# Moving four products with 1/l, a copy and a normalisation within the issue order of VectorE and ScalarE, in a fused attention and recurrent layer

## The chip, the cores and the metric

The kernel runs on one core of a Trainium2 chip. The metric is the device time of one execution in microseconds (us), lower is better. A profile is one execution recorded by the hardware profiler.

## What is computed

The input x has 32 batch elements of 256 tokens with 128 features. First comes an attention layer with 16 heads of 64, causal, with four learned key and value rows ahead of the tokens, then a gated recurrence over the 32 batch elements. Both have a layer norm before them and a residual sum behind them.

```python
# attention, on h = rms_norm(layernorm(x)) * norm_weight
q, k, v = split(h @ w_qkv.T)              # q and k are rotated (rope)
k, v = concat([persist_mem, k]), concat([persist_mem, v])
attn = softmax(where(causal, q @ k.T * 64 ** -0.5, min))
x = x + (attn @ v) @ w_out.T
# recurrence over t = 0..31, on z = layernorm(x)
f, i = sigmoid(z[t] @ wf.T + c @ uf.T + bf), sigmoid(z[t] @ wi.T + c @ ui.T + bi)
c = f * c + i * tanh(z[t] @ wc.T + c @ uc.T + bc)
x = x + tanh(z @ wo.T + c_final @ uo.T + bo)
```

## The kernel before, in words

**Iterations and steps.** Each engine runs its own list of instructions; semaphores tie the lists together. Every list is `body(j, p)` for j = 0 to 34, and each body has eight steps s = 0 to 7, one for each pair of heads. Four batch elements are in work at once. In iteration j the element j is projected and rotated, and its scores for the row maxima are made. Element j - 1 has its transposed scores, exponentials and products with V. Element j - 2 is divided by the softmax sums l, projected by w_out, added to x and normalised for the second layer. Element j - 3 goes through the recurrence's gates. The order of the calls in a step is written out by hand and is the order in which the engine takes them; an engine whose next instruction waits does nothing else.

**TensorE's list** (`body`, L1211), by step: `project(j, s)` (six matmuls, L971, the first instructions of each step with the exception of a transpose in steps 3 and 7); at step 0 `transpose_xn` (L1130), which waits for the second norm; at step 5 `transpose_x` (L938); at step 6 `values(j, 0)` (L990), which waits for `h_lo_done` and fills `ps_work`; at steps 5 and 6 `project_out` for two quarters each (L1115). Quarter n waits for product n + 1 of the element with 1/l (`norm_done`): `project_out(j-2, 0)` and `(1)` in step 5, `(2)` and `(3)` in step 6. Then in each step the scores for the maxima (L1010), the transposed scores (L1034 to L1061), and `attend(j-1, s-1)` (L1078), the product with V. `attend` writes the one bank `ps_pv`, so it waits for `raw_done`, the copy of the pair before it.

**ScalarE's list** (L626): in step s, behind the copies that open some steps, `exp(j-1, s)` (L535), then `hi(j, s-1)`, the fp16 copy of the rotated pair (L520), which waits for GpSimd's `rope_add(j, s-1)`; then `raw_copy(j-1, s-1)` (L560), the copy of `ps_pv`, which waits for `attend(j-1, s-1)`; in step 7 `second_norm(j-2)` (L616) comes last. It waits for the factors that GpSimd's `rstd` makes (L404 to L410). `h_high(j+1)` (L471) stands at the head of step 5.

**VectorE's list** (L864): in step s `rotate(j, s)` (L770 and L771, products with cos and sin out of PSUM), then at step 5 `h_low(j+1)` (L714), which waits for `h_high`, then `maxima` (L781). `divide(j-2, n)` (L817) multiplies two pairs of `raw` by `rinv`, both in SBUF. Products 0 and 1 stand at the end of step 4, behind `state(j-3, 1)` (L858); products 2 and 3 at the end of step 5. The factors 1/l are spread by DMAs (`spread_linv`, L298) into `rinv`.

**GpSimd's list** (L412): in step s `rope_add(j, s-1)` (L396), which adds the two rotated parts when a DMA on the sync engine's queue (`swap`, L280) has swapped the rows of one; in step 7 `rstd(j-2)`; then `prob_add(j-1, s)` (L389), behind the exponential of the step. All of these read SBUF.

Of the kernel before, what the change touches and what calls it, by code (L numbers as in the profile page):

```python
# [5 lines left out]
NB, NT, D = 32, 256, 128  # L6
# [3 lines left out]
NPAIR = NH // 2  # L10
# [41 lines left out]
def build(nc, x, x_last, w_qkv_t, w_out_t, norm_w, pm_k, pm_v, ffn_w, ffn_b, bo_row, consts_f32, consts_cast,  # L52
# [9 lines left out]
    with ctx:  # L62
# [135 lines left out]
        def real(b):  # L198

            return not isinstance(b, int) or 0 <= b < NB  # L200
# [245 lines left out]
        def _(act):  # L446
# [179 lines left out]
            def body(j, p):  # L626
                a, b, c, d = real(j), real(j - 1), real(j - 2), real(j - 3)
                for s in range(NPAIR):
                    if s == 3 and b:
                        copy_top(j - 1, 1)  # L630
                    if s == 7 and a:
                        copy_top(j, 0)
                    if s == 4 and real(j + 4):
                        load_batch(j + 4)
                    if s == 0 and d:
                        xt_high(j - 3)
                    if s == 1 and d and j - 3 == NB - 1:
                        gate_tanh_last(j - 3)
                    elif s in (1, 2) and d and j - 3 < NB - 1:
                        gate_tanh(j - 3, s - 1)  # L640
                    if s < 2 and j == 1:
                        end_values(s)
                    if s in (3, 4) and b:
                        value_copy(j - 1, s - 1)
                    if s == 5 and real(j + 1):
                        h_high(j + 1, 1 - p)
                    if s == 6 and a:
                        value_copy(j, 0)
                    if s == 7 and a:
                        value_copy(j, 1)  # L650
                    if b:
                        exp(j - 1, s)
                    if s == 0 and b:
                        hi(j - 1, NPAIR - 1)
                    if s >= 1 and a:
                        hi(j, s - 1)
                    if s == 1 and b:
                        end_keys(j - 1, 1)
                    if s == 6 and a:
                        end_keys(j, 0)  # L660
                    if s == 0 and c:
                        raw_copy(j - 2, p, NPAIR - 1)
                    if s >= 1 and b:
                        raw_copy(j - 1, 1 - p, s - 1)
                    if s == 2 and real(j + 1):
                        first_norm(j + 1)
                    if s == 5 and d:
                        state_high(j - 3)
                    if s == 7 and c:
                        second_norm(j - 2)  # L670
                    if j == 0 and s == 4:
                        mask_cast()
                    if isinstance(j, int) and j == 1 and s == 4:
                        late_casts()
# [15 lines left out]
        def _(dve):  # L690
# [173 lines left out]
            def body(j, p):  # L864
                a, b, c, d, n = real(j), real(j - 1), real(j - 2), real(j - 3), real(j + 1)
                for s in range(NPAIR):
                    if j == 1 and s == 6:
                        scan_starts()
                    if a:
                        rotate(j, s)  # L870
                    if s == 1 and c:
                        end_add(j - 2, p)
                    if s == 0 and d:
                        xt_low(j - 3)
                    if s == 5 and n:
                        h_low(j + 1, 1 - p)
                    if s < 3 and b:
                        maxima(j - 1, s + 5)
                    if s >= 3 and a:
                        maxima(j, s - 3)  # L880
                    if j == 0 and s == 5:
                        end_low()
                    if s == 0 and n:
                        first_stats(j + 1)
                    if s == 1 and c:
                        invert(j - 2)
                    if s == 3 and c and j - 2 == NB - 1:
                        divide(j - 2, p, 0)
                        divide(j - 2, p, 1)
                    if s == 3 and d:  # L890
                        state(j - 3, 0)
                    if s == 4 and d:
                        state(j - 3, 1)
                    if s == 4 and c and j - 2 == NB - 1:
                        divide(j - 2, p, 2)
                        divide(j - 2, p, 3)
                    if s in (4, 5) and c and j - 2 < NB - 1:
                        divide(j - 2, p, 2 * (s - 4))
                        divide(j - 2, p, 2 * (s - 4) + 1)
                    if s == 6 and b:  # L900
                        end_sum(j - 1)
                    if s == 6 and c:
                        residual(j - 2)
                    if s == 6 and d:
                        state(j - 3, 2)
# [447 lines left out]
```

## Time and profile before

| | us |
|---|---|
| median of three runs | 1214.92 |
| lowest and highest run | 1210.53, 1221.25 |
| the profiled execution, whole | 1218.01 |
| its span, first to last instruction | 1216.1 |
| TensorE busy in it | 1105.0 (91%) |
| VectorE busy | 963.7 (79%) |
| ScalarE busy | 694.0 (57%) |
| GpSimd busy | 639.3 (53%) |

The span and the whole of the profiled execution differ by what lies before the first and behind the last instruction. In the rows below, PE is TensorE, DVE is VectorE, ACT is ScalarE and POOL is GpSimd. A row of the timeline gives the start, the duration, the engine, the line, the operation and the tiles; "x2" are two instructions merged; the brackets at its end give the engine's idle time just ahead of it and what released it. A step of TensorE is read from the start of its first L971 to the start of the next step's first L971.

### The profile page before, as it was taken

How to read it: one execution, taken by the hardware profiler on the slowest of the kernel's cores; microseconds unless marked ns; L12 is line 12 of the kernel's file. 1: busy time of each engine (PE TensorE's matmuls, PEld its weight loads, DVE VectorE, ACT ScalarE, POOL GpSimd, SP SyncE). 2: the span in 40 equal slices, each digit the busy share in tenths (PEclk: the TensorE clock that was granted, in tenths of full speed). 3: DMA queues.
4: the chain of work that ended last, by engine and by line, in shares of the span. 5: the costliest groups of instructions: out<-in, count | busy, mean ns of one | idle time of the engine just before them, and what ended most of it. 6: DMA issues, size and time to landing. Idle time of an engine off the chain costs nothing.

```text
span 1216.1 us, 47269 instructions
## 1 busy us (share of the span) xinstructions
PE 1105.0 (91%) x18411; PEld 829.1 (68%) x18411; DVE 963.7 (79%) x3304; ACT 694.0 (57%) x1603; POOL 639.3 (53%) x828
## 2 busy tenths in 40 slices
PE   3879999999999999999999999999999999989982
PEld 2557767777777777677677777677777777767761
DVE  6677878878888878878778877788888889878536
ACT  3555556556556556656556565565656565555534
POOL 3545555555546555555555555455655555454415
PEclk8899999999999999999999999999999999999995
DMA  5232333333233333323333322333333233333104
GB/s 199 84 93 81 102 106 102 107 107 96 81 99 110 98 107 109 99 73 105 106 99 107 107 83 87 99 107 108 107 106 93 78 107 97 101 103 102 49 21 138
DMA packets 78031, 120.52 MB, mean 99 GB/s; under 512 B 13041, under 2 KB 35954, under 8 KB 77682
## 3 DMA queue, kind: packets, MB, share of 16 engines
q1 hardware_dynamic: 68722, 111.21, 30.0%
q10 hardware_dynamic: 9088, 6.29, 1.8%
q8 instruction: 147, 2.41, 0.9%
q14 instruction: 74, 0.61, 0.2%
HBM read 41.56 MB, written 8.78 MB: 41 GB/s over the span
## 4 chain that ended last, share of the span: by engine, by line
PE 33%; DMA 20%; DVE 17%; issue 8%; POOL 8%; SPq 7%; ACT 6%; DVEq 0%; POOLq 0%; ACTq 0%
DMA rope_c<-rope_b 15%; POOL qk L396 5%; PE bank_pv L1078 5%; DVE raw L817 5%; PE bank_st L1034 5%; SPq L298 4%; PE bank L971 4%; DMA linv_scratch<-linv 4%; DVE masked L781 4%; PE bank_sum L1115 4%; DVE linv L804 4%; PE bank_sm L1010 3%; PE bank L993 2%; ACT xn L616 2%; PE bank_sum L1099 2%
## 5 line engine op out<-in xcount | busy, mean ns | idle before, releaser
L396 POOL TENSOR_TENSOR qk<-rope_a,rope_c 128x512 f32<-128x512 f32 x256 | 341.2, 1333 | 291.6 <-DMA rope_c<-rope_b 279.2
L781 DVE CUSTOM_DVE_ANT_0 masked<-bank_sm,mask_q 128x132 bf16<-128x132 f32 (+1 forms) x1024 | 308.2, 356 | 41.2 <-PE bank_sm L1010 37.6
L389 POOL TENSOR_TENSOR prob<-prob 128x264 f32<-128x264 f32 x256 | 201.3, 786 | 235.7 <-ACT prob L535 229.3
L535 ACT ACTIVATE prob<-bank_st 128x784 f32<-128x784 f32 x256 | 210.3, 822 | 166.4 <-PE bank_st L1043 165.6
L770 DVE TENSOR_TENSOR rope_a<-bank,cos 128x512 f32<-128x512 f32 x256 | 174.1, 680 | 108.2 <-PE bank L971 91.8
L1078 PE MATMUL bank_pv<-prob,v_sb 128*64 128x256 f32 (+1 forms) x2048 | 225.4, 341 | 6.7 <-issue 5.9
L520 ACT ACTIVATE qk_h<-qk 128x512 f16<-128x512 f32 x256 | 159.8, 624 | 118.4 <-POOL qk L396 118.1
L1034 PE MATMUL bank_st<-qk 64*64 64x196 f32 (+3 forms) x4096 | 186.4, 299 | 0.1
L1034 PEld LDWEIGHTS bank_st<-qk 64*64 64x64 f32 x4096 | 167.7, 133 | 9.0 <-issue 0.8
L771 DVE TENSOR_TENSOR rope_b<-bank,sin 128x512 f32<-128x512 f32 x256 | 173.7, 678 | 0.0
L1078 PEld LDWEIGHTS bank_pv<-prob,v_sb 128*64 128x64 f32 x2048 | 125.5, 136 | 60.5 <-issue 8.5
L1115 PE MATMUL bank_sum<-wo_sb,raw 128*128 128x128 f32 x1024 | 133.7, 280 | 17.8 <-DVE raw L817 16.3
L971 PE MATMUL bank<-h_hi,w_hi 128*128 128x256 f16 x512 | 143.7, 281 | 2.7 <-DVE rope_b L771 1.8
L1115 PEld LDWEIGHTS bank_sum<-wo_sb,raw 128*128 128x128 f32 x1024 | 121.5, 191 | 35.8 <-DVE raw L817 34.2
L971 PE MATMUL bank<-h_hi,w_lo 128*128 128x256 f16 x512 | 142.0, 277 | 0.0
L971 PE MATMUL bank<-h_lo,w_hi 128*128 128x256 f16 x512 | 141.8, 277 | 0.0
L817 DVE SCALAR_TENSOR_TENSOR raw<-rinv,raw 128x512 f32<-128x512 f32 x124 | 112.0, 944 | 5.9 <-DMA rinv<-linv_scratch 5.9
L569 ACT ACTIVATE v_sb<-bank 128x512 f32<-128x512 f32 x128 | 76.7, 599 | 50.2 <-PE bank L993 37.5
L1010 PE MATMUL bank_sm<-qk_h 64*64 64x68 f16 (+3 forms) x2048 | 86.8, 246 | 13.9 <-ACT top_t L550 10.4
L560 ACT ACTIVATE raw<-bank_pv 128x256 f32<-128x256 f32 x256 | 94.9, 371 | 0.7 <-PE bank_pv L1084 0.7
L1010 PEld LDWEIGHTS bank_sm<-qk_h 64*64 64x64 f16 x2048 | 38.0, 105 | 81.0 <-issue 64.4
L781 DVE DVE_READ_ACCUMULATOR2_ANT top<- 128x1 f32 x1024 | 84.4, 82 | 0.1
(202 smaller groups left out, 1790.9 us busy)
## 6 DMA issues: line engine op xcount, KB each, us to landing
rope_c<-rope_b SPq DMA_DIRECT2D x512, 128.0 KB, 2.1
rinv<-linv_scratch SPq DMA_DIRECT2D x124, 256.0 KB, 4.6
out<-x_sb SPq DMA_DIRECT2D x16, 256.0 KB, 2.5
linv_scratch<-linv SPq DMA_DIRECT2D x62, 64.0 KB, 2.1
x_sb<-x ACTq DMA_DIRECT2D x28, 128.0 KB, 5.1
pre<-w_qkv_t ACTq DMA_DIRECT2D x1, 1024.0 KB, 5.3
v_sb<-pm_v SPq DMA_DIRECT2D x64, 8.0 KB
v_end<-v_end_scratch SPq DMA_DIRECT2D x64, 8.0 KB
```

The source lines that it names most:

```text
L389: G.tensor_tensor(prob_2[:, s % 4, :, :], prob[:, s % 4, :, 0:NT - Q1], prob[:, s % 4, :, C0 + Q1:SCOL], ALU.add).then_inc(S["prob_added"], 1)
L396: G.tensor_tensor(qk[:, s, :].rearrange("p (u n) -> p u n", u=2)[:, :, 0:NT], rope_a[:, (NPAIR * j + s) % 3, :].rearrange("p (u n) -> p u ...
L535: A.activation(prob[:, s % 4, :, :], ps_st[:, :, 0:SCOL], ACT.Exp).then_inc(S["exp_done"], 1)
L770: V.tensor_tensor(rope_a[:, (NPAIR * j + s) % 3, :], proj_bank(j, s)[:, :], cos[:, :], ALU.mult)
L771: V.tensor_tensor(rope_b[:, s % 2, :], proj_bank(j, s)[:, :], sin[:, :], ALU.mult).then_inc(S["qk_read"], 1)
L781: ins = V.tensor_tensor_reduce(masked[:, e, c0:c0 + n], ps_sm[:, e, c0:c0 + n], mask_q[:, c0:c0 + n], 1.0, LOWEST, ALU.add, ALU.max, top[: ...
L817: V.scalar_tensor_tensor(o, rinv[:, 2 * n:2 * n + 2, :], 1.0, o, ALU.mult, ALU.mult).then_inc(S["norm_done"], 1)
L971: last = T.matmul(proj_bank(j, s)[:, u * NT:(u + 1) * NT], W[q][:, col:col + P], H[p][:, par, NPM:NKEY], start=(i == 0), stop=(i == 2))
L1010: last = T.matmul(ps_sm[OWN[SIDE[qb]], e, c0:c0 + n], qk_h[OWN[e], s, qb * HB:qb * HB + HB], qk_h[OWN[e], s, NT:NT + n], start=True, stop= ...
L1034: T.matmul(ps_st[OWN[SIDE[kb]], e, st_cols(blk)], qk[OWN[e], s, NT + kb * HB:NT + kb * HB + HB], qk[OWN[e], s, q0:NT], start=(kc == 0), st ...
L1078: last = T.matmul(ps_pv[OWN[e], q0:NT], v_sb[:, kc, col:col + DH], prob[:, s % 4, e, c0:c0 + NT - q0], start=(kc == 0), stop=(kc == 1))
L1115: last = T.matmul(ps_sum[:, NT + q * D:NT + (q + 1) * D], raw[:, par, s, q * P:(q + 1) * P], wo_sb[:, s, :], start=(alone and s == 0 and q ...
```

## The change

On ScalarE `raw_copy` goes ahead of `hi` in every step, and `second_norm` in step 7 goes ahead of both. On VectorE the products 2 and 3 go from the end of step 5 to directly behind `rotate`, ahead of `h_low` and `maxima`. The products 0 and 1 stay in step 4 and go ahead of `state(j-3, 1)`. For the last element (j - 2 = NB - 1), whose products read PSUM, products 2 and 3 also go ahead of `state`. No instruction is added, removed or changed, and TensorE's, GpSimd's and the sync engine's lists are the same.

```diff
@@ ScalarE, body
                     if b:
                         exp(j - 1, s)
+                    if s == 7 and c:
+                        second_norm(j - 2)
+                    if s == 0 and c:
+                        raw_copy(j - 2, p, NPAIR - 1)
+                    if s >= 1 and b:
+                        raw_copy(j - 1, 1 - p, s - 1)
                     if s == 0 and b:
                         hi(j - 1, NPAIR - 1)
@@
-                    if s == 0 and c:
-                        raw_copy(j - 2, p, NPAIR - 1)
-                    if s >= 1 and b:
-                        raw_copy(j - 1, 1 - p, s - 1)
                     if s == 2 and real(j + 1):
                         first_norm(j + 1)
                     if s == 5 and d:
                         state_high(j - 3)
-                    if s == 7 and c:
-                        second_norm(j - 2)
@@ VectorE, body
                     if s == 0 and d:
                         xt_low(j - 3)
+                    if s == 5 and c and j - 2 < NB - 1:
+                        divide(j - 2, p, 2)
+                        divide(j - 2, p, 3)
                     if s == 5 and n:
                         h_low(j + 1, 1 - p)
@@
-                    if s == 4 and d:
-                        state(j - 3, 1)
                     if s == 4 and c and j - 2 == NB - 1:
                         divide(j - 2, p, 2)
                         divide(j - 2, p, 3)
-                    if s in (4, 5) and c and j - 2 < NB - 1:
-                        divide(j - 2, p, 2 * (s - 4))
-                        divide(j - 2, p, 2 * (s - 4) + 1)
+                    if s == 4 and c and j - 2 < NB - 1:
+                        divide(j - 2, p, 0)
+                        divide(j - 2, p, 1)
+                    if s == 4 and d:
+                        state(j - 3, 1)
```

## Rows read from the trace of the kernel before

**Rows 1.** The span cut in stretches: busy time by engine, granted clock, DMA share.

```profile
500.00:900.00 400.00, 379.75 (x6454) 287.57 (x6454) 327.20 (x1148) 236.27 (x551) 218.17 (x283) 1.00 0.33 99
```

**Rows 2.** Waits of TensorE, whole span: waiter, releaser, us in total, times, longest.

```profile
PE bank L1130 <- ACT xn L616: 21.4, 31, 2.2
PE bank_sum L1115 <- DVE raw L817: 16.3, 37, 1.2
...
PE bank_pv L1078 <- issue: 5.9, 7, 1.9
```

**Rows 3.** Timeline of TensorE, steps 5 and 6 of the iteration from 603.65.

```profile
625.09 0.28 PE L971 MATMUL bank<-h_hi,w_hi 128*128 128x256 f16 x1
...
629.52 0.88 PE L1078 MATMUL bank_pv<-prob,v_sb 128*64 128x256 f32 x8 [0.57 <-issue]
630.33 0.28 PE L971 MATMUL bank<-h_hi,w_hi 128*128 128x256 f16 x1
...
630.99 0.38 PE L990 MATMUL bank<-w_hi,h_hi 128*128 128x512 f16 x1
...
633.76 1.16 PE L1115 MATMUL bank_sum<-wo_sb,raw 128*128 128x128 f32 x8 [0.52 <-DVE raw L817]
...
636.95 0.27 PE L971 MATMUL bank<-h_hi,w_hi 128*128 128x256 f16 x1
```

**Rows 4.** Timeline of TensorE: start and end of a short step 6.

```profile
559.08 0.28 PE L971 MATMUL bank<-h_hi,w_hi 128*128 128x256 f16 x1
...
564.37 0.27 PE L971 MATMUL bank<-h_hi,w_hi 128*128 128x256 f16 x1
```

**Rows 5.** Timeline of ScalarE, the fp16 copy of step 4, iteration from 603.65.

```profile
628.51 0.63 ACT L520 ACTIVATE qk_h<-qk 128x512 f16<-128x512 f32 x1 [3.66 <-POOL qk L396]
```

**Rows 6.** Timeline of VectorE, steps 4 and 5 of the iteration from 603.65.

```profile
624.57 1.29 DVE L817 SCALAR_TENSOR_TENSOR raw<-rinv,raw 128x512 f32<-128x512 f32 x2
...
627.81 0.68 DVE L771 TENSOR_TENSOR rope_b<-bank,sin 128x512 f32<-128x512 f32 x1
629.82 0.48 DVE L714 SCALAR_TENSOR_TENSOR h_lo<-bank,nw,h_hi 128x256 f16<-128x256 f32 x1 [1.33 <-ACT h_hi L471]
...
631.34 2.36 DVE L817 SCALAR_TENSOR_TENSOR raw<-rinv,raw 128x512 f32<-128x512 f32 x2
```

**Rows 7.** Timeline of GpSimd, `prob_add` in step 5 of that iteration.

```profile
628.43 0.75 POOL L389 TENSOR_TENSOR prob<-prob 128x264 f32<-128x264 f32 x1
```

**Rows 8.** Timelines of VectorE and GpSimd in step 5 of the iteration from 285.29.

```profile
306.88 0.68 DVE L771 TENSOR_TENSOR rope_b<-bank,sin 128x512 f32<-128x512 f32 x1
...
310.31 2.93 DVE L817 SCALAR_TENSOR_TENSOR raw<-rinv,raw 128x512 f32<-128x512 f32 x2
...
307.40 0.76 POOL L389 TENSOR_TENSOR prob<-prob 128x264 f32<-128x264 f32 x1
...
310.27 0.75 POOL L389 TENSOR_TENSOR prob<-prob 128x264 f32<-128x264 f32 x1 [0.88 <-ACT prob L535]
```

**Rows 9.** TensorE, start of that iteration's step 6; VectorE, products from 558.93.

```profile
310.00 0.28 PE L971 MATMUL bank<-h_hi,w_hi 128*128 128x256 f16 x1
...
558.93 1.84 DVE L817 SCALAR_TENSOR_TENSOR raw<-rinv,raw 128x512 f32<-128x512 f32 x2
```

**Rows 10.** TensorE's start of the latest step 5; VectorE's last `rotate` product in it.

```profile
1086.62 0.28 PE L971 MATMUL bank<-h_hi,w_hi 128*128 128x256 f16 x1
...
1090.64 0.68 DVE L771 TENSOR_TENSOR rope_b<-bank,sin 128x512 f32<-128x512 f32 x1
```

**Rows 11.** GpSimd, ScalarE and TensorE around the start of the iteration from 640.87.

```profile
640.45 0.20 POOL L410 TENSOR_TENSOR sx_m<-sx_m,sx_r 128x2 f32<-128x2 f32 x1
...
641.11 0.87 ACT L616 ACTIVATE xn<-x_sb,sx_m,sx_r 128x128 f32<-128x128 f32 x2
...
640.87 0.28 PE L971 MATMUL bank<-h_hi,w_hi 128*128 128x256 f16 x1
...
642.03 0.44 PE L1130 MATMUL bank<-ident_f,xn 128*128 128x128 f32 x2 [0.33 <-ACT xn L616]
```

## The prediction

> **What bounds the kernel now.** I read the stretches first. In the steady part TensorE is busy for 379.75 of 400 us at a granted clock of 1.00 (2.4 GHz), VectorE for 327.20 and the others for about 60% or less [rows 1]. So TensorE's list sets the time, and only idle time inside that list can be won. TensorE's waits name three places: the transposes behind the second norm, `project_out` behind the products with 1/l, and `attend` with a release that the profile does not name [rows 2].
>
> Ends of matmuls are modelled, so I measured by starts: a step lasts from its first L971 to the next step's. For the 28 iterations from 108.1 to 1103.7 the mean is 35.56 us. Steps 1, 2, 4 and 7 repeat to 0.05 us, so they hold no wait that varies. The others:
>
> - Step 6: 19 of 28 last 6.48 to 6.62 us (one: 630.33 to 636.95 [rows 3]), three about 5.75, six 5.29 (one: 559.08 to 564.37 [rows 4]). The mean is 6.20, so 0.91 us an iteration is waiting for products 2 and 3. The reader sees the second such wait in the L1115 row [rows 3].
> - Step 5: 4.59 us in most, mean 4.92. Of the 0.33 us, 0.23 lies ahead of `attend` (L1078) and 0.1 ahead of L1115.
> - Step 0: 4.18 us in 18 of 28, mean 4.49. The transposes begin 1.16 us into the step (640.87 to 642.03 [rows 11]) where without a wait they could at 0.66, as L990 does in step 6 [rows 3]. So even the 18 hold 0.50 us, and the mean wait is 0.8.
>
> **Step 5, the raw copy.** In the iteration of rows 3, `hi(3)` stands in front of `raw_copy(3)` and waits 3.66 us for GpSimd's sum [rows 5]; `attend(4)`, which overwrites the bank that this copy reads, starts at 629.52 and should start 0.57 earlier [rows 3]. The copy could run at 628.51 - 3.66 = 624.85, where ScalarE's wait begins. I take away the 0.23 for all, and half of the 0.1, since products 0 and 1 come 0.34 us earlier: **-0.28 us**. What is now queued behind the copy is `hi`, which in each step waits for the end of `attend` instead, about 0.7 us later than now. It is read two steps later by the scores for the maxima, some 7 us; that slack hides it. If the slack were gone it would cost the same 0.7 us in each step.
>
> **Step 6, products 2 and 3.** They now stand behind `h_low`, which waits 1.33 us for `h_high`, and behind the maxima, and end at 633.70 [rows 6], when `project_out(3)` is wanted at about 633.1. In the new order they begin at the end of `rotate(5)`, 628.41 (the next instruction starts 0.08 ahead of the recorded end of 628.49 [rows 6]), that is 2.9 us earlier. Their factors 1/l have landed by at the latest 1.5 us into step 5 in all 28, and `rotate(5)` ends no sooner than 2.15. So every wait of step 6 for them goes: **-0.91 us**.
>
> What is late next is `h_low`. `values` in step 6 (L990) wants it 0.66 us into the step [rows 3], so 5.25 us into step 5 with step 5 at 4.59. It takes 0.48 and ends 0.08 before the next [rows 6]. Its start depends on how long the two products take. Alone the pair takes 1.29 [rows 6]. But beside GpSimd's sums the same pair takes 1.84 [rows 9], 2.36 [rows 6] or 2.93 [rows 8]: it stands while a sum of GpSimd runs and the other way round, in turn, and 2.93 is the case in which GpSimd starts 0.04 us ahead (310.27 against 310.31 [rows 8]), 1.84 that in which VectorE starts ahead. In the new place GpSimd runs `prob_add(4)` and `rope_add(4)` back to back in nearly every iteration, so the pair will meet them. The Trainium skill, page "SBUF — State Buffer", section "Who interferes with whom", says that a VectorE instruction with two SBUF inputs and a GpSimd one that reads SBUF exclude each other for the whole instruction, whichever issues first going first. The durations in these rows agree with it. If the two did not exclude each other, the sum below would be 5 us lower.
>
> Three kinds of iterations, by the end r of `rotate(5)`, counted from the step's start:
>
> - 10 with r near 2.2. Here `prob_add` has begun before: 307.40 against 307.48 [rows 8]. The pair takes 2.93 - 0.04, ends at 310.37, `h_low` at about 310.8; wanted at 310.00 + 0.66 [rows 8, 9]. A wait of 0.2 in seven, none in the three where GpSimd is 0.1 to 0.3 earlier still.
> - 9 with r from 2.6 to 2.93, and 3 near 3.3. A DMA, the swap of pair 3, releases both engines, and they meet within 0.02 us: VectorE's next could start at 628.41, GpSimd's starts at 628.43 [rows 6, 7]. I take VectorE first, since it is the earlier one by the records. The pair takes 1.84, `h_low` ends at r + 2.2, and is waited for by r - 3.0: nothing in the nine, 0.3 in the three.
> - 6 others: two where the step's products 0 and 1 were held up (0.05 and 0.4), and four where the swap is very late, r from 4.0 to 4.7 (the last: 1090.64 + 0.68 - 1086.62 = 4.70 [rows 10]): 1.0, 1.1, 1.3 and 1.7.
>
> Sum 1.4 + 0.9 + 0.45 + 5.1 = 7.9 over 28: **+0.28 us**. `maxima(2)` ends 1.1 us behind `h_low`, 6.7 into step 5 in the first two kinds, and its bank is wanted at 7.8, later where L990 waits. `rotate(6)` starts about 2 us earlier than now, which lets its swap start earlier too.
>
> **Step 0, the second norm.** At 641.11 it starts behind `hi` and `raw_copy`, while its factors were there at 640.65 [rows 11]. In front it starts at 640.68, 0.43 us sooner. In 10 of the 28 the factors come later than the copies end; there it wins only what the earlier `rotate(6)` gives the swap and the sums behind it, between 0 and 0.3. I take 0.43 in 18 and nothing in 10: **-0.28 us**. With 0.3 in the ten and 0.5 in the 18 it would be -0.43. `raw_copy(6)` now waits for GpSimd in those ten; the bank is wanted 1.3 us behind the transposes, so that is covered. `hi(6)` and `xt_high` behind it are 0.3 to 0.7 late, with over 2 us to spare before the gates of step 1.
>
> **No cost.** Putting `state(1)` behind products 0 and 1 delays it by 1.29; its result is wanted a step later. The list of DMAs is the same, none is issued from the two engines' moved parts. The last element's exchange touches one step.
>
> **Sum.** -0.28 - 0.91 + 0.28 - 0.28 = -1.19 us an iteration. About 30 iterations have all four elements in work, so -36 us: 1218.0 for the profiled execution becomes 1182. The median of the runs lies 3 us under that execution; the forecast is rounded between the two bases to 1181.
>
> **Rivals.**
> (a) GpSimd goes first where the two meet within 0.02 us. Then the pair takes 2.93 instead of 1.84 in 15 iterations, and `h_low` is waited for in all: nine times 0.8, three times 1.35, three times 2.3, the others as before: 21.3 over 28 = 0.76 instead of 0.28. That is -0.71 an iteration, -21 us, **1195**. For it: the 0.02 us is within what the records can tell. Against it: the rows' order. The page of the Trainium skill named above would let either happen, as the first to issue wins.
> (b) No change. The wait moves to the swap chain: GpSimd idles long for swaps, and four steps 5 had `rotate` late by 2 us. If a faster TensorE made the swaps of steps 6 and 7 late as often as step 3's, ten iterations more of about 1 us in step 0 and a longer `h_low` wait of 0.8 would eat it: **1210**. Against: `rotate(6)` moves forward, not back, relative to the end of the iteration.
> (c) Slower: `h_low` as late in every iteration as in the worst one with GpSimd first, 4.70 + 3.3 = 8.0, a wait of 2.75 instead of 0.28. Then +2.75 - 1.47 = +1.28, +38 us, **1256**. It decides from a mean wait of 1.47 on, so from `h_low` ending 6.7 us into step 5 on average; r would have to average 3.4 with GpSimd first, and it averages 2.8.
> (d) The clock falls as TensorE gets busier. It stays at 1.00 with 95% busy [rows 1]; folded into (b).
>
> **Chances.** Forecast 0.58, (a) 0.25, (b) 0.12, (c) 0.05. A difference within 1% is about what a measurement of this kernel can tell from none; the bound is 1202.8. The forecast and (a) are faster by more, though (a) at its weak end and (b) at its strong one cross: faster 0.84, same 0.11, slower 0.05. The range reaches from 1168 (no `h_low` wait and the full gain in step 0: -0.28 - 0.91 - 0.43 = -1.62, -49 us, 1169) to 1200, past (a).
>
> **What the profile would show.** Step 6 by starts near 5.3 us and no L1115 wait there; a new wait of L990 on `h_lo` L714; L1078's wait of 5.9 us gone; L1130's halved, with POOL as what it waits for; the pair of products at 1.84 or 2.93 right behind L771. A `hi` (L520) that L1010 waits for would prove the slack wrong. A long row of L990 waits, over 20 us, would mean (a).

## The result and the profile after

The changed kernel takes 1162.99 us (median of 4 runs, 1161.81 to 1168.67) against 1217.66 us (median of 4, 1210.53 to 1221.25) on the same chip: a ratio of 0.9567, 95% interval 0.951 to 0.9625. That is 4.3% faster. The forecast was 1181 with a range from 1168 to 1200, so the direction was right and the gain was half as large again as forecast: 54.7 us between the medians, 55.1 between the two profiled spans (1216.1 and 1161.0), where the sum had 36. Two of the twenty runs of the first two experiments below went through at a granted clock of 0.66 and 0.56 instead of 0.98 (1528.65 and 1755.99 us); they are left out of the medians.

The page of the kernel after, its first rows:

```profile
span 1161.0 us, 47269 instructions
...
PE 1088.0 (94%) x18411; PEld 826.2 (71%) x18411; DVE 951.9 (82%) x3304; ACT 707.2 (61%) x1603; POOL 649.2 (56%) x828
```

The instructions are the same in number. TensorE lost idle time, as forecast. (Its recorded busy time falls too, from 1105.0 to 1088.0 us for the same instructions. The ends of matmuls are modelled, so I compare starts.) The waits of TensorE after the change, of the places that [rows 2] names (line numbers of TensorE's code are 3 higher, so L1118 is L1115 of before, L1133 is L1130, L993 is L990, L1013 is L1010):

```profile
PE bank L1133 <- ACT xn L616: 8.0, 9, 2.0
PE bank L993 <- DVE h_lo L714: 7.5, 11, 1.2
...
PE bank_sm L1013 <- ACT top_t L550: 1.5, 4, 0.7
...
PE bank_sum L1118 <- DVE raw L817: 0.5, 1, 0.5
```

The reader is to see three things. The products with 1/l are no longer waited for (16.3 us before, 0.5 now), and `attend`'s wait without a named releaser has left the list. `h_low` (L714) is a new wait, as forecast. And the last but one row, the scores for the maxima behind `copy_top`, had 10.4 us before; no term of the forecast had it:

```profile
PE bank_sm L1010 <- ACT top_t L550: 10.4, 29, 1.2
```

The means over the same 28 iterations, by the starts of each step's first matmul, from both traces and from the forecast:

| step | before | after | change | forecast |
|---|---|---|---|---|
| 0 | 4.49 | 3.88 | -0.61 | -0.28 |
| 3 | 3.62 | 3.33 | -0.29 | 0 |
| 5 | 4.92 | 4.60 | -0.32 | -0.28 |
| 6 | 6.20 | 5.65 | -0.55 | -0.63 |
| 1, 2, 4, 7 | 16.32 | 16.32 | 0 | 0 |
| iteration | 35.56 | 33.77 | -1.78 | -1.19 |

28 x 1.78 is 49.9 us. The rest of the 55.1 lies ahead of the iteration that started at 108.1 and now starts at 105.8 (2.3 us), and behind the last of the 28 (3.0 us). Steps 5 and 6 came out at -0.87 against -0.91. By this table steps 0 and 3 hold the miss; the experiments below show that the steps are not independent. A second profile of the changed kernel, taken later, has 3.90, 3.35, 4.60 and 5.52 in these four steps and 33.68 in the iteration, so a difference of 0.1 us in one step between two profiles says little.

**Steps 5 and 6 after.** VectorE, GpSimd and TensorE in the iteration from 614.5, to be laid beside [rows 3, 6 and 7]:

```profile
636.25 0.68 DVE L771 TENSOR_TENSOR rope_b<-bank,sin 128x512 f32<-128x512 f32 x1
636.85 1.83 DVE L817 SCALAR_TENSOR_TENSOR raw<-rinv,raw 128x512 f32<-128x512 f32 x2
638.61 0.47 DVE L714 SCALAR_TENSOR_TENSOR h_lo<-bank,nw,h_hi 128x256 f16<-128x256 f32 x1
...
636.90 1.25 POOL L389 TENSOR_TENSOR prob<-prob 128x264 f32<-128x264 f32 x1
...
638.39 0.28 PE L974 MATMUL bank<-h_hi,w_hi 128*128 128x256 f16 x1
...
643.78 0.27 PE L974 MATMUL bank<-h_hi,w_hi 128*128 128x256 f16 x1
```

The pair starts right behind `rotate(5)`, takes 1.83 us, and GpSimd's `prob_add` is the one that gets longer (1.25 instead of 0.75): VectorE went first. In 24 of the 28 iterations the pair is 0.68 + 1.24 us, in the other four, in which a sum of GpSimd had started ahead, it takes 2.4 to 3.0 us from start to end. Step 6 lasts 643.78 - 638.39 = 5.39 here.

**Step 3.** ScalarE and TensorE around its start, kernel before:

```profile
652.88 0.63 ACT L520 ACTIVATE qk_h<-qk 128x512 f16<-128x512 f32 x1 [0.22 <-POOL qk L396]
653.41 0.37 ACT L560 ACTIVATE raw<-bank_pv 128x256 f32<-128x256 f32 x1
653.68 0.87 ACT L607 ACTIVATE xn<-x_sb,sh_m,sh_r 128x128 f32<-128x128 f32 x2
654.44 0.49 ACT L550 ACTIVATE top_t<-bank_sm 128x128 bf16<-128x128 f32 x3
...
653.38 0.27 PE L971 MATMUL bank<-h_hi,w_hi 128*128 128x256 f16 x1
...
655.08 0.34 PE L1010 MATMUL bank_sm<-qk_h 64*64 64x68 f16 x8 [0.23 <-ACT top_t L550]
```

and after:

```profile
625.70 0.39 ACT L560 ACTIVATE raw<-bank_pv 128x256 f32<-128x256 f32 x1
625.98 0.62 ACT L520 ACTIVATE qk_h<-qk 128x512 f16<-128x512 f32 x1
626.50 0.87 ACT L607 ACTIVATE xn<-x_sb,sh_m,sh_r 128x128 f32<-128x128 f32 x2
627.27 0.49 ACT L550 ACTIVATE top_t<-bank_sm 128x128 bf16<-128x128 f32 x3
...
626.44 0.27 PE L974 MATMUL bank<-h_hi,w_hi 128*128 128x256 f16 x1
...
627.91 0.34 PE L1013 MATMUL bank_sm<-qk_h 64*64 64x68 f16 x8
```

Behind the two copies of step 2 ScalarE has the first norm (L607) and `copy_top` (L550), and TensorE's L1010 waits for the latter. Counted from the step's start, `copy_top` starts at 1.06 before and 0.83 after: the raw copy now fills time in which the fp16 copy waits for GpSimd. L1010 starts at 1.70 before and 1.47 after.

**Step 0.** ScalarE, GpSimd and TensorE, after, beside [rows 11]:

```profile
647.36 0.88 ACT L616 ACTIVATE xn<-x_sb,sx_m,sx_r 128x128 f32<-128x128 f32 x2
648.15 0.36 ACT L560 ACTIVATE raw<-bank_pv 128x256 f32<-128x256 f32 x1
...
647.13 0.20 POOL L410 TENSOR_TENSOR sx_m<-sx_m,sx_r 128x2 f32<-128x2 f32 x1
...
647.70 0.28 PE L974 MATMUL bank<-h_hi,w_hi 128*128 128x256 f16 x1
...
648.37 0.38 PE L1133 MATMUL bank<-ident_f,xn 128*128 128x128 f32 x2
```

The norm starts 0.34 us ahead of the step, 0.24 behind it before, and the transposes follow the projection at 0.67 without a wait. GpSimd's factors end 0.37 ahead of the step; in [rows 11] they ended 0.22 ahead. That second shift was not in the sum.

### The profile page after: what moved, and what is told of

Read it like the earlier page. It is cut to its first block, busy times and chain, and to the rows that moved or that the text cites. A ratio compares the mean times of both kernels' runs of the same rounds, so it can differ in the third digit from the quotient of the medians.

```text
span 1161.0 us, 47269 instructions
## 1 busy us (share of the span) xinstructions
PE 1088.0 (94%) x18411; PEld 826.2 (71%) x18411; DVE 951.9 (82%) x3304; ACT 707.2 (61%) x1603; POOL 649.2 (56%) x828
## 4 chain that ended last, share of the span: by engine, by line
PE 57%; DVE 15%; DMA 14%; SPq 5%; issue 4%; POOL 4%; ACT 2%; DVEq 0%; POOLq 0%; ACTq 0%
PE bank_pv L1081 10%; DMA rope_c<-rope_b 10%; PE bank L974 9%; PE bank_st L1037 7%; PE bank_sum L1118 6%; PE bank_sum L1102 4%; PE bank_sm L1013 4%; DMA linv_scratch<-linv 3%; DVE masked L781 3%; PE bank L996 3%; SPq L298 2%; DVE linv L804 2%; PE bank L993 2%; PE bank L1204 2%; PE bank L1206 2%
## 5 line engine op out<-in xcount | busy, mean ns | idle before, releaser
L389 POOL TENSOR_TENSOR prob<-prob 128x264 f32<-128x264 f32 x256 | 212.0, 828 | 157.6 <-ACT prob L535 150.7
L1118 PEld LDWEIGHTS bank_sum<-wo_sb,raw 128*128 128x128 f32 x1024 | 121.8, 192 | 5.5 <-DVE raw L817 0.9
L1118 PE MATMUL bank_sum<-wo_sb,raw 128*128 128x128 f32 x1024 | 125.1, 275 | 0.5 <-DVE raw L817 0.5
L817 DVE SCALAR_TENSOR_TENSOR raw<-rinv,raw 128x512 f32<-128x512 f32 x124 | 101.1, 857 | 5.7 <-DMA rinv<-linv_scratch 5.6
L560 ACT ACTIVATE raw<-bank_pv 128x256 f32<-128x256 f32 x256 | 97.7, 382 | 1.4 <-PE bank_pv L1081 0.6
L1013 PE MATMUL bank_sm<-qk_h 64*64 64x68 f16 (+3 forms) x2048 | 86.8, 246 | 5.1 <-ACT qk_h L520 3.1
L1013 PEld LDWEIGHTS bank_sm<-qk_h 64*64 64x64 f16 x2048 | 38.1, 105 | 72.3 <-issue 55.0
```

What stands on the lines that cost most here:

```text
L389: G.tensor_tensor(prob_2[:, s % 4, :, :], prob[:, s % 4, :, 0:NT - Q1], prob[:, s % 4, :, C0 + Q1:SCOL], ALU.add).then_inc(S["prob_added"], 1)
L1013: last = T.matmul(ps_sm[OWN[SIDE[qb]], e, c0:c0 + n], qk_h[OWN[e], s, qb * HB:qb * HB + HB], qk_h[OWN[e], s, NT:NT + n], start=True, stop= ...
L1118: last = T.matmul(ps_sum[:, NT + q * D:NT + (q + 1) * D], raw[:, par, s, q * P:(q + 1) * P], wo_sb[:, s, :], start=(alone and s == 0 and q ...
```

## The experiments

All times of one group of runs are beside the kernel before on the same chip. Step means below are over the same 28 iterations. Two theories came out of the comparison: each edit has its own price, and the prices add; or a chain of fixed length ties the steps, so that what one step wins another gives back. I found the candidate for such a chain by counting from the start of step 1: reciprocal of l, its store, its spread to all partitions, and beside the spread's transfers the swap of pair 3, which releases `rotate(5)`. It lands 17.19 us after the start of step 1 before and 17.37 after, though steps 1 to 4 became 0.30 us shorter. The swap is issued behind `rotate(3)`, which ends 10.47 us after the start of step 1 in both, so what TensorE wins in steps 3 and 4 does not bring the swap forward.

**The raw copy in step 2 alone.**

```diff
                     if b:
                         exp(j - 1, s)
+                    if s == 2 and b:
+                        raw_copy(j - 1, 1 - p, s - 1)
@@
-                    if s >= 1 and b:
+                    if s >= 1 and s != 2 and b:
                         raw_copy(j - 1, 1 - p, s - 1)
```

> The kernel before with one call moved: the raw copy ahead of the fp16 copy in step 2 only. Theory: behind these two ScalarE has the first norm and then the copies of the maxima (copy_top, L550) that TensorE's scores for the maxima of step 3 wait for; the raw copy fills time in which the fp16 copy waits for GpSimd, so copy_top ends about 0.25 us sooner. Step 3, by starts of the projection's first matmul, falls from a mean of 3.62 to about 3.33 and the time by 30 x 0.29 = 9 us, to a ratio near 0.993; all other steps stay. Rival: step 3 became shorter through VectorE (products and maxima out of the way); then this kernel changes step 3 by nothing and the time by nothing.

Measured: 1216.58 us (9 runs) against 1214.42 (25 runs), ratio 1.0012, interval 0.9987 to 1.0037. Nothing was won. The steps are read from one more run of the same kernel.

> The kernel before with the raw copy ahead of the fp16 copy in step 2 alone, for a profile at the full granted clock; its time was the same as the kernel before's. Fixed-chain theory: step 3 is 3.3 to 3.4 instead of 3.62, and steps 5 and 6 together are 0.2 to 0.3 longer than the 11.12 of the kernel before, as rotate(5) ends that much later into step 5. Rival: step 3 itself is unchanged, and copy_top was not what it waited for.

Measured: 1218.64 us, span 1216.8. Step 3 is 3.34 us, so it did get the 0.28 us. Steps 5 and 6 are 5.03 + 6.47 = 11.50, 0.38 longer than before (the kernel with only products 0 and 1 moved, which is as fast as the kernel before, differs from it by 0.16 there), and `rotate(5)` ends 3.09 us into step 5 instead of 2.86. Waits of TensorE in it (L1117 is L1115, L1132 is L1130 of before):

```profile
PE bank L1132 <- ACT xn L616: 20.5, 31, 1.9
PE bank_sum L1117 <- DVE raw L819: 20.0, 47, 1.2
```

The wait for the products grew from 16.3 [rows 2] to 20.0 us. The theory of step 3 holds, my expectation of 9 us does not, and the rows fit the second theory: the step's gain is waited for again two and three steps later.

**The raw copy in all steps, nothing else.** The first two hunks of the change without the lines of `second_norm`.

> The kernel before with the raw copy ahead of the fp16 copy in all steps and nothing else. Theory: step 3 falls by 0.29 us as in the kernel with step 2 alone; step 5 falls by 0.23 (the wait of attend goes), but the products 2 and 3 still end when they did, so step 6 grows by most of those 0.23; net -0.3 to -0.4 us an iteration, -9 to -12 us. Rival: the terms add as in the forecast, -0.29 - 0.23 = -0.52, -16 us, with step 6 unchanged at 6.20.

Measured: 1211.14 us (9 runs) against 1214.42, ratio 0.9973, interval 0.9947 to 0.9999. Step 3 -0.26, step 5 -0.22, step 6 +0.31, step 0 +0.11: an iteration of 35.49 instead of 35.56. It is less than either theory gave. The 0.11 in step 0 I had not seen: in step 7 the raw copy waits for `attend`, and the second norm, still the last in the queue, comes 0.1 us later.

**The second norm alone.**

```diff
                     if b:
                         exp(j - 1, s)
+                    if s == 7 and c:
+                        second_norm(j - 2)
@@
-                    if s == 7 and c:
-                        second_norm(j - 2)
```

> The kernel before with the second norm directly behind the exponential in step 7 and nothing else. Theory: step 0 falls by 0.43 to 0.5 us where GpSimd's factors are there (18 of 28) and by nothing where they are late, since rotate(6) has not moved: mean 4.49 to about 4.20, -8 to -9 us. Rival: the whole 0.61 us by which step 0 fell with all the edits belongs to this one, 3.88, -18 us.

Measured: 1208.95 us against 1214.42, ratio 0.9956, interval 0.9931 to 0.998. Step 0 is 4.18, -0.31 (forecast in the prediction: -0.28). Here too step 6 is longer, 6.39 instead of 6.20, and step 5 a little shorter, 4.83. The wait of ScalarE shows what stands in the way next:

```profile
ACT xn L616 <- POOL sx_m L410: 25.9, 28, 6.0
```

With its own copies out of the way the norm waits for GpSimd's factors in 28 places; this term of the sum was sized right for this edit alone. Only 4 of its 28 steps 0 are at 3.63 us, the shortest length seen; 12 are near 3.8, where the factors end 0.2 us ahead of the step.

**Products 2 and 3 alone.**

```diff
+                    if s == 5 and c and j - 2 < NB - 1:
+                        divide(j - 2, p, 2)
+                        divide(j - 2, p, 3)
                     if s == 5 and n:
                         h_low(j + 1, 1 - p)
```

The two calls at the end of step 5 go.

> The kernel before with the products 2 and 3 ahead of h_low and the maxima in step 5 and nothing else. Theory: step 6 falls from 6.20 to about 5.5 (5.29 and a wait of L990 for h_low of 0.1 to 0.3); step 0 falls by 0.1 to 0.2 through the ten iterations in which the factors come late, because rotate(6) starts 0.3 us earlier before the iteration's end; step 5 stays at 4.9. Sum -0.8 to -0.9, -24 to -27 us. Rival: step 0 is untouched and only step 6 moves, -0.6 to -0.7, about -20 us.

Measured: 1177.71 us against 1214.42, ratio 0.9705, interval 0.965 to 0.976. This edit alone brings 36.7 us, more than both theories and two thirds of the whole. Step 6 is 5.31 (-0.89), step 0 is 4.26 (-0.23), step 5 is 4.72 (-0.20). Its waits of TensorE and of ScalarE:

```profile
PE bank L1133 <- ACT xn L616: 14.3, 31, 1.6
...
ACT xn L616 <- POOL sx_m L410: 7.7, 5, 6.0
```

The transposes wait 14.3 us instead of 21.4 [rows 2] with the second norm where it was. `rotate(6)` ends 6.64 us ahead of the iteration's end (6.05 before), its swap lands 3.51 ahead (2.68 before), and the iterations in which it lands later than 2.9 ahead fall from 12 to 5. So the gain in step 0 beyond the norm's own comes from VectorE: nothing stands between step 5 and `rotate(6)` any more but work. With the norm behind its two copies, though, no step 0 is shorter than 4.17 us: in 22 of 28 the factors end 0.37 us or more ahead of the step, and the norm starts at 0.23 all the same.

**Second norm and products 2 and 3, without the raw copy and without products 0 and 1.** The two diffs above together.

> The changed kernel without two of its four moves: the raw copy stays behind the fp16 copy, products 0 and 1 stay behind state; second norm and products 2 and 3 are moved. Theory of the fixed chain: from the start of step 1 a chain of fixed length (reciprocal of l, its store, its spread to all partitions by DMAs, and the swap of pair 3 beside them, which lands 17.2 us into it in every kernel so far) sets when rotate(5) can run; what steps 3 and 5 lose by the raw copy's move is waited for again in step 6. Then this kernel is as fast as the full change within 5 us, 1163 to 1168: step 3 at 3.58, step 5 at 4.72, step 6 at 5.3, step 0 at 3.8. Rival, the terms add: step 3 and step 5 each lose their gain and step 6 keeps the 5.65 of the full change, so 1163 + 30 x 0.45 = 1177.

Measured: 1167.52 us against 1219.62, ratio 0.959, interval 0.954 to 0.9641; the whole change has 0.9567 (0.951 to 0.9625). Step 3 is 3.56, step 5 4.84, step 6 5.31, step 0 3.79, the iteration 33.82 against 33.77 in the kernel after. The terms do not add. What the raw copy (with products 0 and 1) wins on top, 0.23 us in step 3 and 0.24 in step 5, is nearly all given back as 0.34 us of waiting for `h_low` in step 6 and 0.09 in step 0; by the times, too, this kernel and the whole change can't be told apart. In the other direction, the two edits together take 0.70 us from step 0, where alone they took 0.31 and 0.23: now 23 of 28 steps 0 last 3.63 us. The products bring the factors forward, and the norm is at the head of ScalarE's queue to use them; each without the other leaves part of this unused. In time, 52.1 us together against 5.5 and 36.7 alone.

**Products 0 and 1 ahead of `state(1)` alone.**

> The kernel before with products 0 and 1 ahead of state(1) in step 4 and nothing else. All theories: within 2 us of the kernel before, step 5's waits of L1115 (0.1 us an iteration) at most halved.

Measured: one run, 1216.99 us, beside a median of 1215.88 us: no difference that one run could show. In its profile step 5 is 4.94 us (4.92 before), with 0.5 us in one place of waiting for these products, where there were 1.25 in three.

**The spread cut down, in the old order and with the raw copy moved.** Both leave most of the spread out, so most products take the first element's factors.

```diff
-                        sp.dma_start(rinv[OWN[e], 4 * half:4 * half + 4, :].rearrange("p s n -> p (s n)"),
-                                     src.to_broadcast([64, 4 * NT])).then_inc(spread[half], 16)
+                        n = 64 if cj == 0 else 8
+                        sp.dma_start(rinv[64 * e:64 * e + n, 4 * half:4 * half + 4, :].rearrange("p s n -> p (s n)"),
+                                     src.to_broadcast([n, 4 * NT])).then_inc(spread[half], 16)
```

> The kernel before with the spread of 1/l cut from 64 to 8 rows for each half of the partitions, from the second batch element on; the products are then multiplied by factors of the first element in the other rows, so the output is not the reference's. The order of the work is the same. Fixed-chain theory: the spread's transfers hold up the swap of pair 3; without them it lands about 14 us after the start of step 1 instead of 17.2, rotate(5) ends 2.15 us into step 5 in every iteration instead of 2.86 on average, steps 5 are 4.59 and step 6 stays over 6 since the products still stand behind h_low and the maxima: 15 to 20 us less than the kernel before. Rival: the swap is late because the sync engine's list issues it late, or for transfers of another kind; then its landing stays near 17.

> As the kernel with the small spread (most rows of the products take the first element's factors), with the raw copy ahead of the fp16 copy in all steps. Fixed-chain theory: with the late swap gone, the 0.26 to 0.29 us that the raw copy's move takes from step 3 is no longer waited for in step 6, so this kernel is 8 us faster than the one with the small spread alone, where with the full spread the same move gave 3 us. Rival: the move is worth about 3 us here too, since what takes it back is VectorE's own list.

Measured: 1194.44 us (ratio 0.9806, interval 0.9771 to 0.9841) and 1190.58 us (0.9775, 0.9733 to 0.9818). The start of a step 1 and the `rope_add(3)` that the swap of pair 3 releases, in the kernel before

```profile
430.04 0.28 PE L971 MATMUL bank<-h_hi,w_hi 128*128 128x256 f16 x1
...
447.35 1.27 POOL L396 TENSOR_TENSOR qk<-rope_a,rope_c 128x512 f32<-128x512 f32 x1 [3.58 <-DMA rope_c<-rope_b]
```

and with the small spread

```profile
426.98 0.28 PE L972 MATMUL bank<-h_hi,w_hi 128*128 128x256 f16 x1
...
442.00 1.27 POOL L397 TENSOR_TENSOR qk<-rope_a,rope_c 128x512 f32<-128x512 f32 x1 [1.29 <-DMA rope_c<-rope_b]
```

17.31 us against 15.02 in this iteration. On average the swap lands at 13.90 instead of 17.19, with its issue only 0.7 us sooner: the spread's transfers hold it up. But `rotate(5)` does not end at 2.15; it ends at 3.27. The sum that the swap releases now falls on products 0 and 1 at the end of step 4, and these hold up `rotate(5)`: step 5 is 5.25 us with waits for product 0 and 1 in 16 of 28 iterations, and step 6 is 5.29. So my numbers for the steps were wrong, and the time came out 25 us lower by another distribution. Step 6 has no wait left although the order is the old one. The late swap had held up `hi(3)`, and with it `h_high` behind it on ScalarE; now `h_high` starts 1.09 us into step 5 instead of 3.46, and products 2 and 3 end at 6.94 instead of 7.80, with a step 5 that is 0.33 longer.

The pair tells the two theories of the raw copy apart only in part. With the full spread, steps 5 and 6 together grew by 0.09 us when step 3 lost 0.27; with the small one they stay (10.54 and 10.53) when step 3 loses 0.21. That is the direction of the fixed chain, but 0.09 us is no more than two profiles of one kernel differ by. The move is worth 3.9 us here, near the rival's 3 and not 8; step 0 gives back 0.12 through the late second norm. So the fixed chain is shown for the swap's landing, and for what became of the raw copy's gain it is argued.

**h_low ahead of both products, with its own input early.**

```diff
@@ ScalarE
                     if s == 5 and real(j + 1):
                         h_high(j + 1, 1 - p)
+                    if s == 5 and a:
+                        hi(j, 3)
@@
-                    if s >= 1 and a:
+                    if s >= 1 and s != 4 and a:
                         hi(j, s - 1)
@@ VectorE
+                    if s == 5 and n:
+                        h_low(j + 1, 1 - p)
                     if s == 5 and c and j - 2 < NB - 1:
                         divide(j - 2, p, 2)
                         divide(j - 2, p, 3)
-                    if s == 5 and n:
-                        h_low(j + 1, 1 - p)
```

> The changed kernel with h_high on ScalarE ahead of the fp16 copy hi(3), which waits for the late swap, and h_low on VectorE directly behind rotate(5), ahead of products 2 and 3. h_low then no longer waits for GpSimd's sum nor for the two products and ends 0.4 us behind rotate(5), at 3.5 of 5.25 us on average. Theory: the wait of L990 (0.36 us an iteration in the changed kernel) goes and step 6 becomes 5.3; step 0 gives back some 0.1, since rotate(6) stays where it was and the iteration's end comes earlier: -0.25 an iteration, 1163 to about 1155. Rival: products 2 and 3, now 0.4 us later, are waited for instead, and nothing is won: 1163.

Measured: 1172.60 us against 1219.62, ratio 0.9635, interval 0.9592 to 0.9677: by the medians 9.6 us slower than the kernel after, not 8 faster (measured at different times, and the intervals just overlap; an iteration is 34.19 us against 33.77 and 33.68 in the two profiles of the kernel after). L990 waits no more, but step 0 is 4.34 instead of 3.88, and step 6 is 5.52, not 5.3. Its waits of TensorE (L1135 is L1130 of before, L1023 transposes the row maxima, L1018 of before):

```profile
PE bank L1135 <- ACT xn L616: 17.1, 23, 1.7
...
PE bank_sm L1023 <- DVE top L783: 9.0, 10, 4.3
```

The maxima, which stand behind the pair, are now waited for in 10 places (3 in the kernel after), and the products in 4, for 2.0 us. VectorE and GpSimd in a step 5:

```profile
435.10 0.47 DVE L716 SCALAR_TENSOR_TENSOR h_lo<-bank,nw,h_hi 128x256 f16<-128x256 f32 x1
435.49 2.62 DVE L819 SCALAR_TENSOR_TENSOR raw<-rinv,raw 128x512 f32<-128x512 f32 x2
...
435.13 0.76 POOL L389 TENSOR_TENSOR prob<-prob 128x264 f32<-128x264 f32 x1
435.84 1.72 POOL L396 TENSOR_TENSOR qk<-rope_a,rope_c 128x512 f32<-128x512 f32 x1
```

The pair starts 0.36 us behind `prob_add`, GpSimd is first, and it takes 2.62 us instead of 1.83. `rotate(6)` ends 5.69 us ahead of the iteration's end instead of 6.43, and its swap is late in 21 iterations instead of 6. So the order of the rival (a), GpSimd first, costs time through the late `rotate(6)` in step 0. What the rival had put in step 6, the wait for `h_low`, can't appear here, since `h_low` stands in front of the pair.

**h_low between the two products.** The edit on ScalarE as before; on VectorE product 2, `h_low`, product 3.

```diff
                     if s == 5 and c and j - 2 < NB - 1:
                         divide(j - 2, p, 2)
-                        divide(j - 2, p, 3)
                     if s == 5 and n:
                         h_low(j + 1, 1 - p)
+                    if s == 5 and c and j - 2 < NB - 1:
+                        divide(j - 2, p, 3)
```

> The changed kernel with h_high on ScalarE ahead of hi(3), and h_low on VectorE between product 2 and product 3 of step 5. Theory: product 2 still goes ahead of GpSimd's prob_add (the two meet within 0.02 us and VectorE is first), h_low reads PSUM and passes beside that sum, and product 3 waits only for its rest: the pair with h_low ends at r + 2.0 with r the end of rotate(5), not later than now, and h_low at r + 1.1 instead of r + 2.2. L990's wait (0.36 us an iteration in the changed kernel) goes, step 6 becomes 5.29, rotate(6) is as far ahead of the iteration's end as now, step 0 stays at 3.9: -0.3 an iteration, about 9 us less than the changed kernel. Rival: as with h_low in front of both, product 3 meets rope_add and waits the whole of it; rotate(6) and with it the second norm come late, and nothing is won or some us are lost.

> The changed kernel once more, to compare the kernel with the split products with it on one chip. All theories: 1160 to 1168 us.

`h_low` in the kernel after starts right behind the products, without idle time of VectorE in front of it (638.61 above), so an earlier `h_high` on ScalarE should bring nothing by itself. This half of the edit was not run apart.

Measured side by side: 1154.96 us (ratio 0.9493, interval 0.9457 to 0.9529) against 1163.71 us for the changed kernel (0.9575, 0.9532 to 0.9617), so 8.8 us less, where 9 were expected. The two intervals are 0.0003 apart. The two profiled executions differ by less, 1153.94 against 1157.19 us, an iteration by 0.15 us where 0.3 was expected, so how near the 8.8 came to the 9 is in part luck. VectorE and GpSimd in a step 5:

```profile
426.52 0.68 DVE L819 SCALAR_TENSOR_TENSOR raw<-rinv,raw 128x512 f32<-128x512 f32 x1
427.12 0.48 DVE L716 SCALAR_TENSOR_TENSOR h_lo<-bank,nw,h_hi 128x256 f16<-128x256 f32 x1
427.51 0.84 DVE L819 SCALAR_TENSOR_TENSOR raw<-rinv,raw 128x512 f32<-128x512 f32 x1
...
426.55 1.26 POOL L389 TENSOR_TENSOR prob<-prob 128x264 f32<-128x264 f32 x1
427.77 1.72 POOL L396 TENSOR_TENSOR qk<-rope_a,rope_c 128x512 f32<-128x512 f32 x1
```

Product 2 goes first, `h_low`, which reads PSUM, runs beside `prob_add`, and product 3 waits for the rest of that sum alone, 0.84 us instead of 1.24. The products are done as early as in the kernel after, 5.07 us into step 5 (5.02 and 4.84 there), with `h_low` about a microsecond earlier. Step 6 is 5.34 (in the changed kernel 5.65 in its first profile and 5.52 in the one taken beside this kernel), step 0 the same 3.90 as that of the changed kernel beside it. This is the fastest version measured.

## Why the prediction was right and wrong

The direction, the engine that sets the time and the places of most waits were right. The step that failed is the term of step 0, "-0.28": it gave the earlier `rotate(6)` nothing in the ten iterations with late factors, and it measured -0.61, and -0.70 where the second norm and products 2 and 3 are moved alone. Beside it the sum had nothing for step 3 (measured -0.29), and it added terms that do not add. Without the raw copy and products 0 and 1 the kernel is as fast within the noise (1167.52 us, ratio 0.959 against 0.9567), so the second norm and products 2 and 3 carry the gain: -1.74 of the -1.78 us an iteration, where the prediction had -0.91 for them.

**TensorE's list sets the time, and steps 0, 5 and 6 hold the waits:** right as far as it went, but step 3 had one too. The prediction had the numbers in hand: it left step 3 out of "the others" as if it repeated like steps 1, 2, 4 and 7, though its mean of 3.62 stood above its usual 3.53, and the usual length itself held a wait in every iteration (L1010 behind `copy_top`, 29 times, 10.4 us in total, longer than `attend`'s 5.9 that it did name). A wait that is in every iteration does not show as a spread.

**Step 5, the raw copy (-0.28):** measured -0.32, right. A second step that failed stands beside it: "what is now queued behind the copy is `hi`". I asked only what comes later behind the moved instruction. What comes earlier was queued there too: first norm and `copy_top`, 0.23 us sooner, which is step 3's -0.29. The slack of `hi` was as said; L1010 gained no wait for it (3.1 us in two places, 3.0 before). As an edit by itself the raw copy takes 0.22 from step 5, and products 2 and 3 by themselves take 0.20 from it, which the prediction had not: step 5 has only 0.33 to give. And in the whole change the gains of steps 3 and 5 were worth almost nothing, as the kernel without the raw copy shows.

**Step 6, products 2 and 3 (-0.91) and `h_low` (+0.28):** the waits for the products went (0.5 us left), L990's wait came, at 0.36 us an iteration by starts (0.23 in the second profile), so the term of +0.28 was sized about right. Step 6 "near 5.3 us", among the signs, did not fit this term of the prediction's own. VectorE went first in 24 of 28, as taken for where the two meet, with the pair at 1.24 + 0.68 - 0.08 = 1.84. The kinds of iterations shifted, though: of the 10 with `rotate(5)` ending near 2.2 only 3 are left below 2.4, since the chain from step 1 to the swap of pair 3 did not get shorter when steps 1 to 4 did. That the size still came out near is partly luck. Alone, the edit has almost no wait for `h_low` (5.31 in step 6) and brought 36.7 us, where the prediction's terms for it give -0.63 x 30 = -19.

**Step 0, the second norm (-0.28):** the mis-sized term. As an edit by itself it is -0.31. With the products moved, step 0 falls by 0.61. The prediction had the mechanism, "only what the earlier `rotate(6)` gives the swap", and set it to nothing in the ten late iterations and kept 0.43 as a ceiling in the others; its own strong case was -0.43. Products 2 and 3 alone gave step 0 -0.23, as `rotate(6)` ended 0.6 us further ahead of the iteration's end and the late swaps fell from 12 to 5. The two edits' shares alone, 0.31 and 0.23, make 0.54, but together they give 0.70: a norm at the head of the queue needs early factors, and early factors need a norm that doesn't stand behind copies. The raw copy, with products 0 and 1, takes 0.09 of it back. The ten longest steps 0 fell from a mean of 5.07 to 4.34 us, where the prediction allowed 0 to 0.3 and took nothing; the short ones fell by 0.55, from 4.18 to 3.63, where it took 0.43. One reading was wrong too: `rotate(6)` does not start 2 us earlier but 0.93 (2.80 us into step 6 before, 1.87 after), and ends 0.38 further ahead of the iteration's end.

**Sum.** Of the missing 0.59 us an iteration, 0.29 is step 3, 0.33 step 0, and -0.04 steps 5 and 6. Over the 30 iterations of the sum this is 17.7 of the 19 us that are missing between 36 and 55.1. The range ended at -1.62 an iteration, with step 3 at 0 and step 0 at -0.43 in it; both were passed.

**Rival (a):** did not happen in the mean. Where it did, in the four iterations of the kernel after in which GpSimd was ahead, its price is where it had put it: in the one with the pair at 2.96 us, `h_low` ends 5.90 us into step 5 and step 6 lasts 6.00, while with the pair at 1.84 and `rotate(5)` ending as early step 6 is 5.29. The kernel with `h_low` first adds a second price in step 0, which the rival did not have. **Rival (b)**, the wait moving into the swap chain, did not happen to the whole change. Something like it happened to the raw copy in step 2 alone, with another swap, that of pair 3: 0.28 us won in step 3 and all of it waited for again. **Rival (c)** did not happen. **Rival (d)** did not either: the granted clock is 1.00 from 500 to 900 us in the kernel after too.

**What stays open.** Why a swap takes 2.6 us in most iterations and up to 4.5 in some, with nothing else that the profile names, and so what the last wait of step 0 (8.0 us in 9 places, L1133 above) would take to go. And how much of the raw copy's gain comes back through the chain, and how much through VectorE's own list, since both show as waits in steps 5 and 6 and the differences are near those between two profiles of one kernel.

## What to carry to other kernels

When an instruction that waits is moved back in a queue, list what stands behind it down to the next instruction that TensorE waits for, and look for waits that come in every iteration, which spread and maximum do not show. Before adding the gains of several edits, measure from a fixed point whether a chain of transfers sets the length of the stretch: here a gain ahead of its end was worth almost nothing. Ask too which edits need each other: two that feed one wait from two sides, here 0.31 and 0.23 us alone, gave 0.70 together. And where two engines exclude each other, the order in which they meet can be chosen by what stands between: one instruction that does not take part, in front of the pair, made the pair 0.8 us longer; between the two it took no time of its own, and all three were done in 1.83 us, which is what the pair takes by itself when VectorE is first.

## What the runs showed of the hardware

Which engine starts first sets the price, even by 0.05 us: VectorE's product started at 636.85 and GpSimd's sum at 636.90, and so it went in 24 of 28 iterations, with the pair at 0.68 + 1.24 us. In one iteration the sum started 0.03 us ahead, and the pair took 2.96. With one instruction of 0.4 us in front it turned round, to 2.62 us for the pair. The Trainium skill's rule for this, in "SBUF — State Buffer", section "Who interferes with whom", that the first to issue has the whole instruction and the other blocks, fits all three orders here; `h_low`, which reads one operand from PSUM and one tile and a factor from SBUF, kept its 0.48 us beside a running sum.

The two transfers of 128 KB each between partitions that make the `swap` of pair 3 landed 13.90 us after the start of step 1 when the spread beside it was small and 17.19 when it was whole, though they were issued only 0.7 us later. From issue to landing that is 5.74 us instead of 3.18, so the 1 MB of the whole spread costs the swap some 2.6 us. `rotate(5)` waits for this swap (it starts 0.12 us behind the landing in 24 of 28 iterations of the kernel after); with the small spread it waited for products 0 and 1 instead and ended no earlier.
